# Query, key and value projections of a two-expert layer: one masked stream and a weight difference in place of two masked streams

## The reference, cut to what matters

```
def expert_mask(tt):
    vm = jnp.zeros(tt.shape, dtype=bool)
    vm = vm.at[:, :-1].set((tt[:, :-1] == 1) & (tt[:, 1:] == 1))
    return vm
...
vm = expert_mask(token_type_ids)[..., None]
residual = hidden_states
x = rms_norm(hidden_states, ln_in_w)
mixed = jnp.where(vm, x @ v_qkv, x @ l_qkv)
q, k, v = jnp.split(mixed, 3, axis=-1)
q, k, v = (heads(q, NH, HD), heads(k, NH, HD), heads(v, NH, HD))
q, k = apply_rotary(q, k, position_ids, l)
```

## Time and profile before

| | |
|---|---|
| median of 3 runs | 2162.44 us |
| the profiled execution: its own time | 2162.32 us |
| the profiled execution: its span | 2159.6 us (2.7 us lie around it) |
| TensorE matmul / VectorE / ScalarE / GpSimd busy | 92% / 70% / 47% / 24% of the span |
| the stage, 356 to 601.5 us | 245.5 us |
| TensorE busy in the stage | 212.3 us |
| mean granted TensorE clock over the span | 0.955 |

### The profile page before, as it was taken

One profiled execution on the slowest core, in us unless ns is written; L12 is line 12 of the kernel. 1 busy time (PEld: TensorE's weight loads), 2 busy tenths in 40 slices (PEclk: granted clock), 3 DMA queues, 4 the chain that ended last, 5 costly groups with the idle time before them and its releaser, 6 DMA issues. The chain is left out here.

```text
span 2159.6 us, 32786 instructions
## 1 busy us (share of the span) xinstructions
PE 1990.5 (92%) x12637; PEld 1335.5 (62%) x12654; DVE 1520.9 (70%) x2111; ACT 1009.4 (47%) x1752; POOL 510.8 (24%) x496
## 2 busy tenths in 40 slices
PE   7899997899889997888789999999998899999997
PEld 5788875777745555666534444444434677878885
DVE  5676786788857775556589999999942566766563
ACT  1232313555425553444358888888883222221111
POOL 0321231244301223322101322323232222221211
PEclk9999999899969999999879999999999999999999
DMA  3222021433477743776635435345301333334331
GB/s 140 71 100 81 21 72 59 143 123 123 142 181 171 179 120 109 241 234 218 166 76 92 85 78 99 69 88 88 84 17 46 107 93 99 104 105 117 93 98 56
DMA packets 174793, 236.93 MB, mean 110 GB/s; under 512 B 26218, under 2 KB 103022, under 8 KB 172426
## 3 DMA queue, kind: packets, MB, share of 16 engines
q1 hardware_dynamic: 164368, 222.60, 38.3%
q0 software_dynamic: 7856, 10.90, 1.8%
q10 hardware_dynamic: 2400, 1.12, 0.2%
HBM read 169.54 MB, written 62.91 MB: 108 GB/s over the span
## 5 line engine op out<-in xcount | busy, mean ns | idle before, releaser
L2135 ACT ACTIVATE pT_x<-ps 128x512 f32<-128x512 f32 (+1 forms) x832 | 451.6, 595 | 84.3 <-PE ps L2233 56.8
L2174 DVE TENSOR_REDUCE quarters<-ps 128x2 f32<-128x804 f32 x480 | 454.1, 992 | 45.3 <-PE ps L2205 43.7
L2248 PE MATMUL ps<-pT_x,vx_ring 128*17 128x256 f32 (+1 forms) x3328 | 261.4, 387 | 0.2 <-ACT osb_x L2117 0.2
L105 PE MATMUL ps<-mi_h,w_hi 128*128 128x512 f32 (+1 forms) x440 | 173.8, 395 | 9.7 <-DVE mi_l L2429 9.7
L2394 POOL TENSOR_TENSOR sg<-sg,keep_all 128x512 f32<-128x512 f32 (+1 forms) x55 | 88.0, 1601 | 382.5 <-ACT sg L2373 382.5
L106 PE MATMUL ps<-mi_h,w_lo 128*128 128x512 f32 (+1 forms) x440 | 172.9, 393 | 0.0
L107 PE MATMUL ps<-mi_l,w_hi 128*128 128x512 f32 (+1 forms) x440 | 172.8, 393 | 0.0
L1322 DVE TENSOR_REDUCE row_max_s<-ps 128x1 f32<-128x384 f32 (+3 forms) x176 | 109.5, 633 | 65.4 <-PE ps L1354 64.6
L1294 ACT ACTIVATE pT_s<-ps 128x512 f32<-128x512 f32 (+1 forms) x176 | 96.1, 559 | 113.4 <-PE ps L1379 111.4
L99 DVE CAST w_hi<-w_raw 128x512 fp32r<-128x512 f32 (+1 forms) x165 | 84.3, 511 | 71.5 <-PE ps L107 65.8
L2248 PEld LDWEIGHTS ps<-pT_x,vx_ring 128*17 128x17 f32 (+1 forms) x3328 | 55.6, 95 | 110.9 <-issue 72.6
(11 more groups left out here) (351 smaller groups left out, 4805.2 us busy)
## 6 DMA issues: line engine op xcount, KB each, us to landing
qkv_l<-self_q_by_part SPq DMA_DIRECT2D x48, 256.0 KB, 4.4
qkv_h<-self_k_by_part SPq DMA_DIRECT2D x48, 256.0 KB, 6.6
w_raw<-L_xattn_l_gate SPq DMA_DIRECT2D x40, 256.0 KB, 2.9
w_raw<-L_xattn_l_up SPq DMA_DIRECT2D x40, 256.0 KB, 2.9
w_raw<-L_xattn_l_down SPq DMA_DIRECT2D x40, 256.0 KB, 2.7
kx_first<-cross_k_by_part SPq DMA_DIRECT2D x36, 200.2 KB, 7.0
cross_v_by_group<-v_aug SPq DMA_DIRECT2D x16, 442.0 KB, 3.9
vx_ring<-cross_v_by_group SPq DMA_DIRECT2D x16, 442.0 KB, 9.9
```

What stands on the lines that cost most here:

```text
L105: nc.tensor.matmul(dst, ah, bh, start=start, stop=False, **how)
L2135: nc.scalar.activation(pT[0:kn, u % 3, j, :], ps[0:kn, 5 + v % 3, :], ACT.Exp, scale=SCALE)\
L2174: nc.vector.tensor_reduce(out=quarters[:, g % 2, pair, :, q, quarter], in_=ps[:, at:at + 2, 0:MAXW], axis=AX.X, op=ALU.max)\
L2248: last = nc.tensor.matmul(ps[j * HD:j * HD + CHD + 1, 4, queries], v_r[0:kn, g % RING, kt, j, :], pT[0:kn, u % 3, j, queries], start=kt == ...
```

## The change

The second expert's weight is replaced by the difference of the two weights, D = v_qkv - l_qkv, and the first expert takes the whole stream: x @ l_qkv for all tokens plus (keep_1 * x) @ D. In the kernel:

- `round_x` (ScalarE) rounds `h * w` itself, four times a turn and not eight; `rest_x` (VectorE) forms `h * w - high` in one instruction, four times. `mask_x` multiplies both finished parts by `keep_1`, two VectorE instructions for each of four tiles. The `full` step is gone. In turns 1 to 3 the order is four `rest_x`, then four `mask_x`; `mask_x` waits until TensorE has done the step of the turn before that reads the tile.
- The weights go in 12 pairs p (both experts' tiles of the same k): 24 loads and not 20. VectorE makes the difference in place (`difference`), ScalarE rounds it (`round_difference`), VectorE splits it (`rest_difference`). The ring is two slots for each expert: the first expert's slot is free with `s_df` (the difference is made), the second's with `s_ws` (it is split).
- `keep_columns` stands ahead of piece j = 2 in turns 0 to 2.
- TensorE's matmuls, their shapes and their order stay; it waits for the first expert's weight by `s_df`, for the difference by `s_ws`.

```
@@ -686,7 +686,7 @@
...
+                def raw_slot(p, e):
+                    return 2 * (p % 2) + e
...
@@ -754,10 +758,14 @@
...
-                        for n in range(SPLIT, NT):
-                            g, e, k = GROUPS[n // G], n % G // DT, n % DT
-                            load_w(sp, n - SPLIT, weights[e][k * P:(k + 1) * P, g * D:(g + 1) * D], wl, s["s_ws"])
-                            if n == 2 * G:
+                        for p in range(3 * DT):
+                            g, k = GROUPS[p // DT], p % DT
+                            for e, s_free in enumerate((s["s_df"], s["s_ws"])):
+                                slot = raw_slot(p, e)
+                                if p >= 2:
+                                    sp.wait_ge(s_free, p - 1)
+                                sp.dma_start(w_raw[:, slot, :], weights[e][k * P:(k + 1) * P, g * D:(g + 1) * D]).then_inc(wl[slot], 16)
+                            if p == 2 * DT - 1:
                                 sp.dma_start(fused_d[turns[0]], h[:, :, :]).then_inc(s["s_hup"], 16)
...
-                        def round_w(n):
-                            act.wait_ge(wl[n % RAW], 16 * (n // RAW))
-                            nc.scalar.activation(split_of(n)[0], w_raw[:, n % RAW, :], ACT.Copy).then_inc(s["s_wh"], 1)
...
-                            act.wait_ge(s["s_x"], 2 * DT * i + n + 1)
...
+                            act.wait_ge(wl[raw_slot(p, 0)], 16 * (p // 2 + 1))
+                            nc.scalar.activation(split_of(G * (p // DT) + p % DT)[0], w_raw[:, raw_slot(p, 0), :], ACT.Copy).then_inc(s["s_wh"], 1)
+                        def round_difference(p):
+                            act.wait_ge(s["s_df"], p + 1)
+                            nc.scalar.activation(split_of(G * (p // DT) + DT + p % DT)[0], w_raw[:, raw_slot(p, 1), :], ACT.Copy)\
+                                .then_inc(s["s_wd"], 1)
...
+                        def round_x(i, k):
                             if i:
-                                act.wait_ge(s["s_wu"], NT * (i - 1) + 2 * G + n + 1)
-                            nc.scalar.activation(xe[e][0][:, k, :], full[:, n % 2, :], ACT.Copy).then_inc(s["s_xh"], 1)
+                                act.wait_ge(s["s_hin"], 16 * i)
+                                act.wait_ge(s["s_wu"], NT * (i - 1) + 2 * G + k + 1)
+                            nc.scalar.activation(xe[0][0][:, k, :], h[:, k, :], ACT.Copy, scale=w_both[:, k:k + 1]).then_inc(s["s_xh"], 1)
...
@@ -880,13 +893,15 @@
...
-                        for n in range(2 * DT):
-                            round_x(0, n)
-                            if n >= SPLIT:
-                                round_w(n)
-                        for n in range(2 * DT):
-                            square(0, n // DT, n % DT)
-                            round_w(G + n)
+                        for k in range(DT):
+                            round_x(0, k)
+                        for p in range(DT):
+                            round_difference(p)
+                            square(0, 0, p)
+                        for p in range(DT, 2 * DT):
+                            round_w(p)
+                            square(0, 1, p - DT)
+                            round_difference(p)
...
@@ -898,8 +913,9 @@
...
-                                for n in range(2 * G, 3 * G):
-                                    round_w(n)
+                                for p in range(2 * DT, 3 * DT):
+                                    round_w(p)
+                                    round_difference(p)
                             keep_plain(i, 0)
...
@@ -910,7 +926,8 @@
...
                                 for n in range(2 * DT):
-                                    round_x(i + 1, n)
+                                    if n < DT:
+                                        round_x(i + 1, n)
                                     square(i + 1, n // DT, n % DT)
...
@@ -970,31 +987,54 @@
...
-                        def rest_w(n):
-                            hi_, lo_ = split_of(n)
-                            dve.wait_ge(s["s_wh"], n - SPLIT + 1)
-                            nc.vector.tensor_tensor(out=lo_, in0=w_raw[:, n % RAW, :], in1=hi_.bitcast(f32), op=ALU.subtract)\
+                        def rest_w(p):
+                            hi_, lo_ = split_of(G * (p // DT) + p % DT)
+                            dve.wait_ge(s["s_wh"], p - DT + 1)
+                            nc.vector.tensor_tensor(out=lo_, in0=w_raw[:, raw_slot(p, 0), :], in1=hi_.bitcast(f32), op=ALU.subtract)
+                        def difference(p):
+                            for e in range(2):
+                                dve.wait_ge(wl[raw_slot(p, e)], 16 * (p // 2 + 1))
+                            second = w_raw[:, raw_slot(p, 1), :]
+                            nc.vector.tensor_tensor(out=second, in0=second, in1=w_raw[:, raw_slot(p, 0), :], op=ALU.subtract)\
+                                .then_inc(s["s_df"], 1)
+                        def rest_difference(p):
+                            hi_, lo_ = split_of(G * (p // DT) + DT + p % DT)
+                            dve.wait_ge(s["s_wd"], p + 1)
+                            nc.vector.tensor_tensor(out=lo_, in0=w_raw[:, raw_slot(p, 1), :], in1=hi_.bitcast(f32), op=ALU.subtract)\
                                 .then_inc(s["s_ws"], 1)
-                        def mask_x(i, n):
-                            e, k = divmod(n, DT)
...
-                                dve.wait_ge(s["s_xl"], o - 1)
-                            if n == 0 and i:
...
+                        def rest_x(i, k):
+                            dve.wait_ge(s["s_xh"], DT * i + k + 1)
+                            nc.vector.scalar_tensor_tensor(out=xe[0][1][:, k, :], in0=h[:, k, :], scalar=w_both[:, k:k + 1],
+                                                           in1=xe[0][0][:, k, :].bitcast(f32), op0=ALU.mult, op1=ALU.subtract)\
+                                .then_inc(s["s_xl0"], 1)
+                        def mask_x(i, k):
+                            if k == 0 and i:
                                 dve.wait_ge(s["s_k"], NK * i)
-                                dve.wait_ge(s["s_hin"], 16 * i)
-                            nc.vector.scalar_tensor_tensor(out=full[:, n % 2, :], in0=h[:, k, :], scalar=w_both[:, k:k + 1],
-                                                           in1=keeps[i % 2][:, e, :], op0=ALU.mult, op1=ALU.mult).then_inc(s["s_x"], 1)
-                        def rest_x(i, n):
-                            e, k = divmod(n, DT)
-                            dve.wait_ge(s["s_xh"], 2 * DT * i + n + 1)
-                            nc.vector.tensor_tensor(out=xe[e][1][:, k, :], in0=full[:, n % 2, :],
-                                                    in1=xe[e][0][:, k, :].bitcast(f32), op=ALU.subtract).then_inc(s["s_xl"], 1)
+                            if i:
+                                dve.wait_ge(s["s_wu"], NT * (i - 1) + 2 * G + DT + k + 1)
+                            dve.wait_ge(s["s_xl0"], DT * i + k + 1)
+                            for part in range(2):
+                                last = nc.vector.tensor_tensor(out=xe[1][part][:, k, :], in0=xe[0][part][:, k, :].bitcast(f32),
+                                                               in1=keeps[i % 2][:, 1, :], op=ALU.mult)
+                            last.then_inc(s["s_xl1"], 1)
...
@@ -1027,7 +1067,7 @@
                             dve.wait_ge(s["s_tab"], 5 * (i + 1))
                             for j in range(DT + 1):
                                 o = 2 * DT * i + DT * group + j
-                                if (j, group) == ((DT - 1, 0) if i < B - 1 else (2, 1)):
+                                if (j, group) == ((2, 0) if i < B - 1 else (2, 1)):
                                     keep_columns(i)
...
@@ -1046,33 +1086,29 @@
...
-                        for n in range(2 * DT + 1):
-                            if n < 2 * DT:
-                                mask_x(0, n)
-                            if n:
-                                rest_x(0, n - 1)
-                                if n > SPLIT:
-                                    rest_w(n - 1)
-                        for n in range(G, 2 * G):
-                            rest_w(n)
+                        for k in range(DT):
+                            rest_x(0, k)
+                        for p in range(DT):
+                            difference(p)
+                            mask_x(0, p)
+                            rest_difference(p)
+                        more_weights(DT)
                         for i in range(B):
                             if i:
...
                             if i == 0:
-                                for n in range(2 * G, 3 * G):
-                                    rest_w(n)
+                                more_weights(2 * DT)
...
                                 find_keep(i + 1)
```

(15 more changed lines are left out.)

16 lines of the change are left out of this document (10 added, 6 removed).

## The result

The changed kernel takes 2168.94 us (median of 5 runs, 2167.76 to 2174.38) against 2161.3 us (2158.8 to 2163.06) in the same comparison: a ratio of 1.0046, 95% interval 1.0034 to 1.0059. That is 7 to 13 us slower by the interval. The profiled execution has a span of 2165.9 us, 6.3 more than before.

What follows compares the result with a forecast made beforehand. It took the chain over ScalarE, GpSimd and VectorE, with VectorE late, to bound the stage, not TensorE. 2162.3 + 5.2 (weights part 1) + 5.3 (part 2) + 3 x 0 (between turns) = 2172.8 us; range 2160 to 2179.

Steps and rivals of the forecast that it cites:

- Part 1 of the weights: Turn 0, up to the first norm: differences wait for loads in rounds of 4.0 us, norm 5.2 us later.
- Part 2: Turn 0, tables to first piece: twelve VectorE instructions and two load rounds take 13.4 us, not 8.1, 5.3 more.
- Between the turns: Three boundaries: VectorE's sequence takes 20.2 us against 19.85, with GpSimd's instructions blocking it; taken as 0.
- rival (a): Between the turns: ScalarE and GpSimd set the time, 2.7 us less at each of three, 2164.7 us; chance 0.16.
- The column copy: Copy of `rs_col` 2.76 us sooner: no gain at the end while VectorE's chain is the longer one.
- TensorE's waits grow: In the turns: TensorE has 50.6 us of work in 54.3 us, waits may lower its clock, off the path.
- The sum: Whole kernel: first piece 10.5 us late, nothing gained or lost between turns, 2172.8 us.
- Rival (b): Stage: added weight work hides in turn 0, VectorE's turn falls below TensorE's; faster, 2151.1 us; chance 0.09.
- Rival (c): Weight loads in turn 0 crowd each other, 3.4 us each and not 2.6: +15.4, 2177.7 us; chance 0.07.

Runs made afterwards that it cites:

- e4_order: The changed kernel with each difference's low part (`rest_difference`) right behind that difference, not behind the next pair's; 2169.33 us, ratio 1.0036.
- e5_ring3: e4_order with a third pair of raw weight slots; 2167.43 us, ratio 1.0032.
- e6_pool: The changed kernel with GpSimd's additions of squares cut to 128 of 512 columns in turns 1 to 3; 2156.23 us, ratio 0.9985.
- e1_columns: The kernel before with one edit, the copy of the norm columns one piece sooner in turns 0 to 2; 2168.36 us, ratio 1.0034.

## Why the prediction was right, point by point

- **Part 1 of the weights, +5.2.** Counted from the beginning of the stage (356.6 before, 354.8 now) the first norm's `exp`, which starts at 385.50 before and at 389.00 now, is 5.3 us later. Right. The cause was right as well (a round of 4.46 us from 379.38 to 383.84 and one of 4.11 in part 2, ended by loads), but the single steps were met less well than their sum: pair 5 waited for no load and came 2.5 us behind pair 4 (3.6 worked out), pair 6 then 5.1 behind it (4.0). That these cancel is luck. And the steps past the ring are the larger share, which e4_order and e5_ring3 showed.
- **Part 2, +5.3.** From that `exp` to the first shuffle: 20.1 us against 14.9, so 5.2. Its differences 8, 10 and 11 and the last split came within 0.2 us of the times worked out, counted from the beginning of the stage.
- **Between the turns, 0.** Measured 20.23 us, worked out 20.2; before, 19.85. That an instruction waits for what is left of GpSimd's was the term that decided between the forecast and rival (a), and e6_pool shows it at two sizes. I had put it at 8 times 1.03 = 8.3 us; measured it is six masks at 1.10, two low parts at 0.55 and 0.3 on the multiply, 8.0. The row of 1.65 that I read as an instruction of 0.68 is one of 0.75 alone; the term doesn't change by it. Rival (a), 2.7 us less, came in no kernel that kept GpSimd's additions and full masks.
- **The column copy, 0.** Right in the changed kernel, but the reason given was not the whole one: I wrote that the earlier start can gain nothing as long as VectorE's chain is the longer one. e1_columns shows that it can lose 7 us, where TensorE comes to its branch too early. That the changed kernel is spared this is luck. I think that TensorE's new waits in turn 0 and for the second sum keep it back; no run takes them away.
- **TensorE's waits grow: half right.** In the stage they went from 19.9 to 27.0 us in all, and the clock of the turns stayed at 0.97 or above. But the ones for the columns didn't grow; they went, and others came at places I didn't name (sum of squares in turn 0, line 876 later). The one for `plain` was named.
- **The sum, +10.5.** The stage is 10.6 us longer from its first instruction (11.3 from TensorE's first product, which comes 0.7 sooner as forecast: it waited 4.36 us in place of 5.03 for its first tile); the ratio gives 7 to 13, the medians 7.6. The two profiled spans differ by 6.3 us only, and the 4.3 us that they have less lie outside the stage: 1.8 us ahead of it and 2.5 behind it. Kernels that don't touch the part behind it spread there from 1555.6 to 1561.4 us, so this is no term of the change.
- **Rival (b), TensorE as the bound.** It put TensorE's turn at 50.6 with half clock behind a wait. e6_pool gives 49.9 at a clock of 1.00. Its condition (a first piece less than 2.8 us late) never came near.
- **Rival (c).** Loads of line 767 take 2.8 us in the median, not 3.4. Its price was mis-added: seven loads at 0.8 more are 5.6 us, not 5, so 2178.4 in place of 2177.7.

## What to carry to other kernels

Work that is done once still stands in a queue: twelve additional steps, each fed by the step before over two engines, cost 7 to 8 us here even with buffers for all of them (GpSimd's share in it isn't taken apart), and no later turn gave that back. Shortening an engine's stream is worth little if its instructions stand beside GpSimd's: count the instructions that meet GpSimd, not their size. And look at what an engine reaches sooner once a wait is gone: here a branch whose 3 us had stood behind queued work.

## What the hardware showed that I had not expected

- Behind TensorE's read of a flag and its branch the next product started no sooner than 4.2 us after GpSimd's last addition, for which the sums ahead of them wait, 1.9 us of sums included, and each time 2.5 us or more behind a packet of 0.02 MB on the instruction queue. That is hidden only if enough products are still queued: 0 us of idle time where 3.7 us of them were, 0.24 with 2.2, 1.17 with 1.2, 3.06 with none.
- Waits of like length don't cost the clock alike: 3.54 us ahead of part 2 left a turn at 0.97, 3.06 us ahead of the second expert's products a turn at 0.88. In e5_ring3 waits of 0.6, 1.9 and 2.1 us in a turn left it at 1.00.
- What GpSimd costs a VectorE instruction with two inputs goes with what is left of GpSimd's instruction, not with VectorE's size: +1.10 us for one of 512 columns on an instruction of 0.68 as on one of 0.28, +0.27 us for one of 128 columns, and +0.55 where the instruction started 0.6 us behind GpSimd's (the low part at 430.50 in the changed kernel, 1.30 us for 0.75). A shuffle, with one input, stayed at 0.73 to 0.76.
